# Probabilities of 64 large attentions: TensorE turns replaced by VectorE 32x32 squares and sixteen on-chip transfers a batch, context sums two slots later

## The reference, cut to what matters

```python
qh = (q_in @ wq + bq).reshape(b, q_len, H, K)          # H = 16, K = 128
kh = (kv_in @ wk + bk).reshape(b, t, H, K)
vh = (kv_in @ wv + bv).reshape(b, t, H, K)
kh = jnp.concatenate([kh, broadcast(bias_k)], axis=1)  # 376th key
vh = jnp.concatenate([vh, broadcast(bias_v)], axis=1)
logits = jnp.einsum('bqhk,bthk->bhqt', qh, kh) / scale
weights = jax.nn.softmax(logits, axis=-1)
ctx = jnp.einsum('bhqt,bthk->bqhk', weights, vh).reshape(b, q_len, H * K)
return ctx @ wo + bo
```

## Time and profile before

| | |
|---|---|
| median of 3 runs | 2303.13 us (2302.65 to 2303.64) |
| span of the profiled execution | 2301.3 us |
| time of the profiled execution around its span | not listed; the median is 1.8 us above this span |
| TensorE busy | 2273.7 us (99%) |
| TensorE weight loads | 2061.8 us (90%) |
| VectorE busy | 1339.3 us (58%) |
| ScalarE busy | 1122.5 us (49%) |
| GpSimd busy | 359.4 us (16%) |
| DMA bytes | 376.25 MB, mean 163 GB/s |

### The profile page before, as it was taken

One profiled execution on the slowest core, in us unless ns is written; L12 is line 12 of the kernel. 1 busy time (PEld: TensorE's weight loads), 2 busy tenths in 40 slices (PEclk: granted clock), 3 DMA queues, 4 the chain that ended last, 5 costly groups with the idle time before them and its releaser, 6 DMA issues.

```text
span 2301.3 us, 37087 instructions
## 1 busy us (share of the span) xinstructions
PE 2273.7 (99%) x13091; PEld 2061.8 (90%) x13091; DVE 1339.3 (58%) x3102; ACT 1122.5 (49%) x2468; POOL 359.4 (16%) x727
## 2 busy tenths in 40 slices
PE   7999999999999999999999999999999999999999
PEld 6777788889999999999998899999999999998887
DVE  6877774524655655665664526565565565564743
ACT  5777753344444445454453434445445445453421
POOL 2111065320000101001002210001001001012421
PEclk9999999999999999999999999999999999999999
DMA  5422135574554755745744554555556556454110
GB/s 196 139 90 104 62 112 195 170 245 134 191 191 151 237 181 166 232 170 181 230 142 146 210 167 147 205 192 184 193 191 198 179 191 213 164 167 132 54 55 33
DMA packets 255224, 376.25 MB, mean 163 GB/s; under 512 B 90302, under 2 KB 205906, under 8 KB 255042
## 3 DMA queue, kind: packets, MB, share of 16 engines
q1 hardware_dynamic: 255042, 373.87, 48.3%
HBM read 315.77 MB, written 58.05 MB: 162 GB/s over the span
## 4 chain that ended last, share of the span: by engine, by line
PE 94%; DVE 3%; ACT 1%; issue 1%; DMA 0%; SPq 0%; DVEq 0%; ACTq 0%
PE ps_k L1766 10%; PE ps_k L1767 10%; PE ps_k L1768 10%; PE ps_o L1766 9%; PE ps_o L1768 9%; PE ps_o L1767 9%; PE ps_v L1766 6%; PE ps_v L1768 6%; PE ps_v L1767 6%; PE ps_s L1766 4%; PE ps_s L1768 4%; PE ps_s L1767 4%; PE ps_t L1963 3%; PE ps_t L1901 2%; PE ps_s L1888 1%
## 5 line engine op out<-in xcount | busy, mean ns | idle before, releaser
L1766 PE MATMUL ps_k<-cs_hi,w_a_hi 128*128 128x376 f32 x1132 | 383.0, 338 | 0.0
L1767 PE MATMUL ps_k<-cs_lo,w_a_hi 128*128 128x376 f32 x1132 | 378.6, 334 | 0.0
L1768 PE MATMUL ps_k<-cs_hi,w_a_lo 128*128 128x376 f32 x1132 | 377.6, 334 | 0.0
L1141 ACT ACTIVATE prob<-ps_s,row_columns 112x376 f32<-112x376 f32 x256 | 147.2, 575 | 304.0 <-DVE row_columns L1538 304.0
L851 POOL CAST k_hi<-xk_hi 128x1 fp32r<-128x1 f32 x256 | 47.0, 184 | 1226.6 <-PE ps_s L1768 1226.6
L1766 PEld LDWEIGHTS ps_k<-cs_hi,w_a_hi 128*128 128x128 f32 x1132 | 213.1, 188 | 1.3 <-issue 0.3
L1767 PEld LDWEIGHTS ps_k<-cs_lo,w_a_hi 128*128 128x128 f32 x1132 | 213.2, 188 | 0.5
L1768 PEld LDWEIGHTS ps_k<-cs_hi,w_a_lo 128*128 128x128 f32 x1132 | 213.2, 188 | 0.0
L1532 DVE SCALAR_TENSOR_TENSOR k_lo<-ps_k,col_b,k_hi 128x375 fp32r<-128x375 f32 x252 | 152.8, 606 | 72.5 <-ACT k_hi L1110 66.9
L1110 ACT ACTIVATE k_hi<-ps_k,col_b 128x375 fp32r<-128x375 f32 x252 | 143.7, 570 | 82.7 <-PE ps_k L1768 81.7
L1423 DVE RECIPROCAL row_columns<-row_columns 112x1 f32<-112x1 f32 x384 | 62.6, 163 | 195.1 <-ACT prob L1141 187.4
(11 more groups left out here) (283 smaller groups left out, 5749.5 us busy)
## 6 DMA issues: line engine op xcount, KB each, us to landing
ckd_hi<-context_by_key_halves SPq DMA_DIRECT2D x64, 768.0 KB, 4.5
ckd_lo<-context_by_key_halves SPq DMA_DIRECT2D x64, 768.0 KB, 6.4
cs_hi<-context_halves SPq DMA_DIRECT2D x64, 752.0 KB, 6.2
cs_lo<-context_halves SPq DMA_DIRECT2D x64, 752.0 KB, 7.9
w_raw_b<-in_blocks_b SPq DMA_DIRECT2D x104, 256.0 KB, 4.1
w_raw_a<-in_blocks_a SPq DMA_DIRECT2D x104, 256.0 KB, 4.3
q<-q_scratch SPq DMA_DIRECT2D x72, 224.0 KB, 6.3
extra<-extra_probability SPq DMA_DIRECT2D x16, 896.0 KB, 5.1
```

The source lines that it names most:

```text
L1141: act.activation(prob[buf][0:LQ, 0:KW], ps_s[buf][0:LQ, 0:KW], ACT.Exp, bias=max_neg[0:LQ, buf:buf + 1], accum_out=prob_sum[0:LQ, buf:buf ...
L1766: pe.matmul(out, w_h, m_h, start=first, stop=False)
L1767: pe.matmul(out, w_h, m_l, start=False, stop=False)
L1768: return pe.matmul(out, w_l, m_h, start=False, stop=last)
```

## The change

In the two large attentions TensorE turns nothing any more. VectorE transposes the normalised probabilities in squares of 32 by 32 into a new tile `blocks` (one buffer), unit by unit. When the fourth unit is in it, SyncE issues 16 transfers from SBUF to SBUF (32 partitions by 384 values each, 48 KB) that bring the squares to their partitions, into the lo tile of `pt`. ScalarE then makes the hi part of the whole batch in one copy of 1536 columns, and GpSimd the lo part in three subtractions of 512 columns. The four sums of a batch come two slots later on TensorE. To make the squares whole, a head has 128 query rows (4 bands of 28 rows and 4 spare), so `q`, scores and softmax work on 128 partitions, and a matmul of the sums reads its 448 columns in runs of 28. `ckd` has one buffer in four parts, each loaded again as soon as its sum is made. Keys alternate between two banks. In the epilogue the first two projection rows come ahead of the last batch's sums.

```diff
-        self.loads = isinstance(self.b, int) and self.b == 1 and not self.head
+        self.loads = isinstance(self.b, int) and self.b == att.loading and (group > 0 or not att.layer and not self.head)
...
-        return {2: (0, 1), 3: (2, 3)}.get(t, ()) if self.att.layer and self.loads else ()
+        return {0: (0, 1), 1: (2, 3)}.get(t, ()) if self.att.layer and self.loads else ()
...
         def chunks(place, t):
...
+            last = place.before()
+            if t >= 2:
+                return () if last is None or outputs_here(place) else ((last, t - 2),)
+            if last is None or last.before() is None:
                 return ()
...
+            return ((last.before(), 2 * t), (last.before(), 2 * t + 1)) if outputs_here(last) else ((last.before(), t + 2),)
...
+                def move_blocks(place):
+                    sp.wait_ge(block_turn, unit_1(place, NT))
+                    wait(sp, c_mm, NT * (place.visit - 1))
+                    sp.sem_inc(sp_waited, 1)
+                    for s in range(4):
+                        for i in range(BANDS):
+                            dst = pt[place.parity][1][SQUARE * s:SQUARE * (s + 1), i * D_BAND:(i + 1) * D_BAND].bitcast(F32)
+                            src = blocks[SQUARE * i:SQUARE * (i + 1), s * D_BAND:(s + 1) * D_BAND]
+                            sp.dma_start(dst, src).then_inc(turned_in[place.parity], 16)
...
+                        if t == 2:
+                            store_extra(place)
+                            move_blocks(place)
...
+                        for summed, d in chunks(place, t):
+                            load_by_key(summed.next(), d)
+                        if t == 1 and place.loads:
+                            load_block(1, place.block_b + 1)
+                            load_block(0, place.block_a + 1)
...
+                def turned_lo(place):
+                    pool.wait_ge(t_hi, place.visit + 1)
+                    for i in range(3):
+                        part = slice(i * D, (i + 1) * D)
+                        hi, lo = (pt[place.parity][s][:, part] for s in range(2))
+                        pool.tensor_tensor(lo, lo.bitcast(F32), hi, ALU.subtract).then_inc(t_lo, 1)
...
+                        if t == 1 and place.before():
+                            turned_lo(place.before())
                         split_lo(1, place.block_b, place.split_own(t))
...
+                def turned_hi(place):
+                    act.wait_ge(turned_in[place.parity], 256 * place.pairs + 256)
+                    act.activation(pt[place.parity][0][:], pt[place.parity][1][:].bitcast(F32),
+                                   ACT.Identity).then_inc(t_hi, 1)
...
                         if place.key(t + 2):
                             exp(*place.key(t + 2))
+                        if t == 0 and place.before():
+                            turned_hi(place.before())
...
+                    normalize(place.unit + t, prob[buf], buf, extra_probability, slice(0, P))
+                    dve.wait_ge(s_norm, place.unit + t + 1)
+                    if t == 0:
+                        if place.before():
+                            dve.wait_ge(turned_in[1 - place.parity], 256 * place.before().pairs + 256)
+                    dve.transpose(blocks[:].rearrange("p (s j t e) -> p t j s e", s=4, j=3, t=NT)[:, t],
+                                  prob[buf][:, 0:BLOCKS * SQUARE].rearrange("p (j s e) -> p j s e", j=3, s=4)).then_inc(block_turn, 1)
...
-                def turn(place, t):
...
-                    for i, (k0, n) in enumerate(KEY_TILES):
-                        last = pe.transpose(ps_t[buf][0:n, i * LQ:(i + 1) * LQ], prob[buf][0:LQ, k0:k0 + n], ident[0:LQ, 0:LQ])
-                    last.then_inc(t_mm, 1)
...
+                def context_sum(place, d):
...
+                        pe.wait_ge(t_lo, 3 * place.visit + 3)
+                    pe.wait_ge(ck_in[d], 16 * place.visit + 16)
...
                 def epilogue(place):
...
+                    for d in (2, 3):
+                        context_sum(place.before(), d)
...
+                    for r in range(EARLY_TILES):
+                        project_row(1, 0, 0, 5 * RT + 4 * RT * a, r, early)
+                    for d in range(DT):
+                        context_sum(place, d)
```

More of the change, by code:

```diff
@@ L432, in key_bank @@
                 return ps_o[0] if place.head and place.parity == 0 and t == 1 else ps_k
-            return ps_o[1] if two_key_banks(place, t) and t % 2 == 0 else ps_k
+            return (ps_k, ps_t[0])[t % 2]
         def two_key_banks(place, t):
@@ L438, in two_key_banks @@
                 return place.head and place.parity == 0 and t == 1
-            return place.head and place.parity == 1 and t < NT - 1
+            return True
         def hidden_place(c, f, half):
@@ L706, in one_batch @@
-                    if place.final:
-                        sp.wait_ge(k_mm, place.tile)
-                        land(0, a, (0, 1))
-                    store_extra(place)
-                    for head in heads(place, 1):
-                        store_head(quad_before(place), head)
-                    if place.quarter == 3:
-                        load_extra(place)
-                    if not place.final and not (place.head and place.parity == 0):
-                        sp.wait_ge(c_mm, NT * place.visit)
-                        sp.sem_inc(sp_waited, 1)
-                        load_by_key(place.next())
@@ L718, in one_batch @@
-                    if place.after(2):
-                        load_q(place.after(2))
-                    if query_piece(place, 3):
-                        last_query(query, a, skip, query_piece(place, 3))
+                    for t in range(NT):
+                        if t == 0 and place.after(2):
+                            sp.wait_ge(k_mm, place.tile + NT)
+                            sp.sem_inc(sp_waited, 1)
+                            load_halves(place.after(2))
+                        if t == 0 and place.final:
+                            sp.wait_ge(k_mm, place.tile)
+                            land(0, a, (0, 1))
+                        if query_piece(place, t):
+                            last_query(query, a, skip, query_piece(place, t))
+                        if t == 1 and place.after(2):
+                            load_q(place.after(2))
+                        if t == 2:
+                            store_extra(place)
+                            move_blocks(place)
+                        if t == 3 and place.quarter == 3:
+                            load_extra(place)
+                        for head in heads(place, t):
+                            store_head(quad_before(place), head)
+                        for summed, d in chunks(place, t):
[3 more added lines that the diff above has]
+                            load_block(0, place.block_a + 1)
@@ L722, in one_batch @@
+                    if place.head and place.parity == 0:
                         all_queries_stored()
-                    if place.loads:
-                        load_block(1, place.block_b + 1)
-                        load_block(0, place.block_a + 1)
                 def epilogue(place):
@@ L731, in epilogue @@
                     load_block(0, place.block_a + 2)
+                    for d in range(2, DT):
+                        load_by_key(place, d)
                     for t in range(NT):
@@ L1586, in prologue @@
                     last_query(query, a, between, FIRST_PIECES)
-                    turned_lo(place, 0)
                 def one_batch(place):
@@ L1690, in project @@
                 more = layer and group + 1 < GROUPS
-                for r in range(RT):
+                for r in range(EARLY_TILES if group == 0 else 0, RT):
                     if norm is None:
@@ L1814, in query @@
                         pe.wait_ge(v_ev, 3)
-                    query_products(slot, query_bank(i, between), t, half, (0, DT))
+                    query_products(layer, slot, query_bank(i, between), t, half, (0, DT))
                     for row in later_rows(norm).get(i, ()):
@@ L2064, in bank_read, with project_row @@
                 wait(pe, x_add, x0 + before + 1)
+            def project_row(layer, group, slot, x0, r, outputs):
+                bank_read(r, x0)
+                for t in range(NT):
+                    last = product(y_bank(layer, group, r)[:], [outputs[s][:, t, r * P:(r + 1) * P] for s in range(2)],
+                                   [w[slot][s][:, t, :] for s in range(2)], t == 0, t == NT - 1)
+                last.then_inc(y_mm, 1)
             def project(layer, a, group, slot, n, step, x0, norm=None):
```

335 lines of the change are left out of this document (140 added, 195 removed).

## The result

The changed kernel takes **2760.23 us** (median of 4 runs, 2758.86 to 2761.89) against 2303.39 for the kernel before (4 runs, 2302.65 to 2304.06): a ratio of 1.1983, 95% interval 1.1966 to 1.2. The forecast was slower, 2398 us with a range of 2285 to 2520. The direction is right and the size is wrong by 362 us.

A forecast was written before the change was run, and what follows sets the result against it. TensorE bounds the kernel before; after the change, VectorE's transpose waiting for the moves bounds ordinary batches. Each attention costs 40 + 9 - 1 = 48 us, both 96; 2301.3 + 96, plus 1.8, gives 2398 us, range 2285 to 2520.

The forecast's parts named there:

- The formula of the batch, 11.9 + M: VectorE's chain between landing and next fourth transpose, 11.9 us, plus M is the shortest batch: 20.4 us.
- M: Time from a batch's fourth transpose to the landing of its last move: 8.5 us, ends 7.4 and 11.1.
- the 7 after these: Steps following head-output steps have two sums in slot 1, the second 2.0 us later: 22.4 us each, 157 together.
- Small transfers ... are issued 0.39 and 0.46 apart: Issue distance from the program's start, used for the 16 moves on one queue: 15 x 0.46 = 6.9 us.
- The prediction's own sign for steps over 21.5 us: If ordinary batches are over 21.5 us apart, look at the transpose's own duration first.
- 7 steps over slots with head outputs are still TensorE's: Per attention, TensorE's work sets the length of head-output steps: 22.9 us each, 160 together.
- 7.2 late, 3 times: Block loads of batch 2, groups 1 to 3, stand ahead of the moves and delay them: 22 us an attention.
- 9 more: At each attention's end, last sums wait for moves and copies, and sums the first batches skipped come there: 9 us more.
- Rival 5: Moves run one after the other at 0.92 us each, M 15.3: about 2740 us, chance 0.04.
- Rival 4: VectorE's transposes take 0.91 us, or moves wait behind other traffic (M 11.1): 2480 to 2530 us, chance 0.20.
- Rival 1: Moves land early and TensorE stays the bound of the batches: 2270 us, chance 0.14.
- The last addition: Span 2301.3 plus 96 for both attentions is 2397; with 1.8 between span and median, forecast 2398 us.

The follow-up runs named there:

- the kernel with three parts: Changed kernel with two buffers, stores of head outputs 0 and 1 ahead of the moves, block loads behind them, ScalarE's copy in three parts: 2367.8 us.
- by way of DRAM: Changed kernel, one buffer, 16 moves replaced by one DRAM write and four reads, head stores between: 2390.37 us; with late loads and copy in three parts 2366.66 us.

## Why the prediction was right and wrong

**Right.** The mechanism: one `blocks` buffer, VectorE's first transpose of a batch held until the last move of the one before lands, 62 times. The formula of the batch, 11.9 + M, gives 23.5 with the measured M, and ordinary steps are 24.0 (23.5 to 25.3). In the batch shown above the 11.9 are 12.35 (1222.49 to 1234.84); the difference is one normalisation that took 0.90 in place of 0.41, of which more at the end. With half of the moves M is 11.6 - 8 x 0.63 = 6.6 and the formula gives 18.5, at the lower end of the measured 18.7 to 21.8. That is weak support: 18.7 is also the ordinary step with two buffers, where no transpose waits, so something else bounds it there. TensorE's own ordinary slot is 4.43 us in the kernel with three parts, against 4.40. ScalarE's large copy is 1.48 against 1.49.

**Wrong, by parts of one attention** (steps of the first, forecast and measured):

| steps | forecast | measured | more |
|---|---|---|---|
| 14 ordinary and split ones | 293 | 338.7 | 46 |
| the first three | 57 | 72.7 | 16 |
| 7 with head outputs, loads in three | 182 | 271.0 | 89 |
| the 7 after these | 157 | 175.2 | 18 |
| sum | 689 | 857.6 | 169 |

- **"Small transfers ... are issued 0.39 and 0.46 apart" failed.** The moves are 0.63 apart and land 1.9 later. M is 11.6, past my upper end of 11.1. That end took 0.6 for the issue without a row for it, and the value rested on two distances between three transfers at the program's start. 3.1 us in 14 ordinary steps are 43 of the 46; they are also 9 of the 16 of the first three steps, of which the other 7 stay open, and would cover the 18 of the 7 steps behind head outputs. The prediction's own sign for steps over 21.5 us pointed at the transpose's duration; that was 0.58, and the excess was in M.
- **"7 steps over slots with head outputs are still TensorE's" failed, and cost most.** I costed these steps by TensorE's work alone, although the formula for the others rests on VectorE's waiting transpose. In the changed kernel, VectorE and then TensorE in such a step:

```profile
1246.65 0.58 DVE L1610 STREAM_TRANSPOSE blocks<-prob 128x384 f32<-128x384 f32 x1 [5.25 <-DMA pt_lo<-blocks]
1247.77 0.62 DVE L1626 TENSOR_TENSOR o<-ps_o,extra 128x448 f32<-128x448 f32 x1 [0.54 <-DMA o_scratch<-o]
```
```profile
1248.54 0.71 PE L1814 MATMUL ps_o<-sums_hi,w_b_hi 128*128 128x448 f32 x1 [4.15 <-DVE o L1626]
1249.05 0.57 PE L1815 MATMUL ps_o<-sums_lo,w_b_hi 128*128 128x448 f32 x1
1249.43 0.57 PE L1816 MATMUL ps_o<-sums_hi,w_b_lo 128*128 128x448 f32 x1
```

  Output 2 stands behind the waiting transpose, TensorE needs its bank, and what follows is at half the clock. I named `key_lo`, `sum_lo` and `maximum` as queued behind that transpose, and left `output` out. The second cause, the stores behind the 16 moves, I didn't see at all: it was hidden by the first, and showed only when the buffer was doubled. I had been through VectorE's queue behind a new wait, and not through SyncE's behind 16 new issues. Not all of the 89 is these two causes. With both gone (two buffers, stores first) such a step is still 28.6 and the one behind it 19.2, where I had 22.9 and 22.4: I had drawn the line between the two kinds of steps wrong by some 3 us. Without loads the two together are 61.2 here, 47.8 with both causes gone and 45.3 in the forecast, so 13.4 us a pair go with the causes and 2.5 stay open.
- **Block loads** ahead of the moves: "7.2 late, 3 times". These steps are 43.5 against 35, so 8.5 each, and their removal gave 45 us over 6 of them, 7.5 each. Right in mechanism and size.
- **The ends of the attentions, "9 more"** and 1 less for the prologue, are 21 each. TensorE's timeline behind the first attention's last mark, and the windows of that stretch (its clock is the 0.86):

```profile
1428.62 0.74 PE L1814 MATMUL ps_v<-pt_hi,ckd 128*128 128x448 f32 x1 [2.96 <-POOL pt_lo L905]
1455.31 0.77 PE L1814 MATMUL ps_o<-w_a_hi,act_t_hi 128*128 128x512 f32 x1 [6.26 <-DVE o L1626]
```
```profile
1410.84:1470.00 59.16, 49.75 (x202) 42.29 (x203) 19.68 (x27) 18.95 (x23) 8.85 (x8) 0.86 0.48 148
1470.00:1624.62 154.62, 153.09 (x748) 136.03 (x747) 67.46 (x115) 65.37 (x122) 34.64 (x35) 1.00 0.51 173
```

  The kernel before, from mark to mark:

```profile
1201.87:1395.19 193.32, 192.40 (x932) 166.61 (x930) 85.20 (x138) 83.54 (x147) 39.61 (x39) 1.00 0.53 174
```

  Before, TensorE was idle for 0.9 us of that whole stretch at full clock. Now it is idle for 9.4 us in its first 59, and 49.75 us of work at 0.86 are some 7 us more than at full clock (an estimate); the two make 16 of the 20.5. I had the chain in the forecast, priced it too low and gave its clock no term. No experiment aimed at this part, but the marks of the others bear on it: with half of the moves the two ends cost 31 us in place of 42, by way of DRAM 32, while with two buffers (44), the stores first, the copy in parts (43) and even the short subtractions (46) they cost as much as before. So the time of the moves is in it, and GpSimd's subtractions are not what sets it.
- **The clock had no term.** For the same 12323 matmuls TensorE is busy 2369.4 us here and 2249.6 in the kernel with three parts, whose mean clock is 0.987 against 0.936. How much of these 120 us lengthened the program, and how much lay in the shadow of the waits, no run separates.
- **Rival 5**, the moves one after another, gave a time near the measured one (2740), by luck, and is wrong: with issues 0.63 apart and landings after 1.9, three are in flight at once, and M is 11.6 and not 15.3.
- **Rival 4's transposes**: 0.578 us for 384 columns, 0.50 from start to start. The plain row of 0.41 was the better guide than the slow one of 0.907. The Trainium skill's 311 ns ("VectorE: DVE Perf Modes", section The three transpose paths) is for 128 x 128 in bf16; three times that, my estimate of 0.93, doesn't hold for this shape.
- **Rival 1**, TensorE the bound at 2270, was never near even with the wait gone: the two kernels closest to it need 2367 us. In the one with three parts the two ends cost 43 us, the steps behind the late loads 24 (4 us in each of 6), and the quads without loads are 84.9 to 86.9 where the turns removed would leave 80.5: at 85.0, 72 for 16 quads. Together 139, an estimate, against 77 of turns saved and 64 of time lost.
- **The last addition**: 2301.3 + 96 + 1.8 is 2399 and not 2398, which changes nothing.

## To carry to other kernels

Count the issues of a transfer pattern before its bytes. Where the trace has no row of the same kind (here none from SBUF to SBUF), the distance between issues is a guess: price the slowest single issue at hand as well (here `w_raw`, median 0.55 us), and ask what the time would be there. Ask when a buffer is free again, not only when its contents arrive: one write that freed the buffer early, with the stores behind it, gave as much as a second buffer with the stores first. For every instruction that will wait, and for every queue that gets a run of new issues, list everything behind it, in each kind of step and not only in the ordinary one. When a chain of waits is broken and little comes back, look at the steps that didn't move: there a second cause stood behind the first, and its remedy (the stores first) has the opposite sign while the first is there.

## What I had not expected of the hardware

- An issue of a transfer of 32 partitions from SBUF to SBUF holds SyncE's queue for 0.63 us from start to start, with 48 KB and with 12 KB; on ScalarE's queue it is about the same (8 in 5.01 us), and keeps ScalarE from computing. Reads from DRAM into 32 partitions, 192 KB each, were 0.44 apart (four in 1.75 us).
- VectorE's normalisation of 375 columns took 0.90 us in place of 0.41 where GpSimd's three subtractions of 512 columns ran beside it (mean of all 256 in the changed kernel 489 ns). VectorE, then GpSimd in the changed kernel:

```profile
1233.33 0.90 DVE L1481 TENSOR_SCALAR prob<-prob,row_columns 128x375 f32<-128x375 f32 x1
```
```profile
1230.26 3.75 POOL L905 TENSOR_TENSOR pt_lo<-pt_lo,pt_hi 128x512 fp32r<-128x512 f32 x3 [5.39 <-ACT pt_hi L1176]
```

  In the kernel with two buffers and the copy in three parts the mean was 419 ns, and with subtractions of 64 columns 406. The Trainium skill, "SBUF — State Buffer", section SBUF: two separate sides, says that GpSimd and a VectorE operation in a two-port mode, or one with two SBUF inputs, take one pair of ports in turn, each for a whole instruction. The end at 1234.23, just behind GpSimd's at 1234.01, fits such a wait roughly (a wait until 1234.01 and then the full 0.41 would end at 1234.42); that this normalisation is of either kind no run shows.
- After 4.15 us in which it had nothing to do, TensorE was granted 0.50 of its clock, 1.2 of 2.4 GHz, over 1248.5 to 1252.5, and matmuls of 448 columns started 0.37 us apart in place of 0.20.
